# GNN layer with a routed mixture of experts: hidden sums kept and split in PSUM, four banks for the first layer, two for the second

## The reference, cut to what matters

```python
x = x + gnn(_layernorm(x), src, dst, edge_weight)       # N = 50000 rows of D = 256
# FFN: E = 8 experts, F = 1024, top-1 routing, capacity C = ceil(1.25 * N / E)
h = _layernorm(x)
probs = softmax(h @ gate_w + gate_b); idx = argmax(probs)
buf = rows of h gathered per expert (at most C each)
hmid = relu(buf @ w1[e] + b1[e])                        # [C, 1024]
ybuf = hmid @ w2[e] + b2[e]                             # [C, 256]
x = x + nan_to_num(ybuf[idx, pos] * prb * kept)
```

## Time and profile before

| what | value |
|---|---|
| median of three runs | 3566.1 us |
| the profiled execution: its own time | 3569.06 us |
| its span in the profile | 3567.3 us |
| mean granted TensorE clock, of full speed | 0.82 |
| PE busy | 2846.6 us (80%) |
| DVE busy | 2245.0 us (63%) |
| ACT busy | 1539.7 us (43%) |
| POOL busy | 1724.4 us (48%) |

### The profile page before, as it was taken

How to read it: one execution, slowest core, us unless ns; L and a number is a source line. 1 busy time by engine, 2 the same in 40 slices (tenths; PEclk the granted TensorE clock), 3 DMA queues, 4 the chain that set the end, 5 groups by cost and what they waited for, 6 DMA issues and landing times.

```text
span 3567.3 us, 60077 instructions
## 1 busy us (share of the span) xinstructions
PE 2846.6 (80%) x18806; PEld 2603.9 (73%) x18807; DVE 2245.0 (63%) x5836; ACT 1539.7 (43%) x2638; POOL 1724.4 (48%) x1183
## 2 busy tenths in 40 slices
PE   4553434067677777499999999999999999999998
PEld 3443433067676667399898999888999989998987
DVE  5645555076566566377666677676677776667666
ACT  2322222044444444255444555454455545554443
POOL 4788887635555566333434333343433343334323
PEclk8666666555555555699999999999999999999999
DMA  8544444388787776311211211121211121111111
GB/s 313 153 89 77 87 78 86 29 269 252 249 259 248 228 240 207 115 48 56 66 57 44 72 48 52 49 67 57 67 48 47 56 67 47 48 51 49 42 47 37
DMA packets 306007, 374.74 MB, mean 105 GB/s; under 512 B 34887, under 2 KB 266340, under 8 KB 302608
## 3 DMA queue, kind: packets, MB, share of 16 engines
q1 hardware_dynamic: 224608, 202.49, 19.3%
q0 software_dynamic: 77728, 145.22, 14.9%
q10 hardware_dynamic: 3600, 26.22, 1.8%
HBM read 185.42 MB, written 196.46 MB: 107 GB/s over the span
## 4 chain that ended last, share of the span: by engine, by line
PE 53%; DVE 4%; issue 1%; DVEq 0%; DMA 0%; SPq 0%; ACT 0%; POOL 0%; POOLq 0%; ACTq 0%
PE u_Y L1181 27%; PE u_H L1170 23%; PE u_T L1153 3%; DVE y L1110 1%; DVE yo L1129 1%; DVE yo L1126 1%; DVE y L1115 0%; DVE hn L1078 0%; DVE low L1120 0%; DVE hlo L1098 0%; DVE yo L1124 0%; DMA slots<-blank 0%; DMA u_pay<-slots 0%; DVE scales L1073 0%; DVEq L1078 0%
## 5 line engine op out<-in xcount | busy, mean ns | idle before, releaser
L1010 POOL DMA_INDIRECT out_x<-yo,u_token x348 | 668.5, 1921 | 1261.4 <-DVE yo L1131 1179.5
L1181 PE MATMUL u_Y<-whi,hhi 128*128 128x256 f32 x2784 | 784.2, 282 | 1.5 <-DVE hlo L1098 1.5
L1181 PE MATMUL u_Y<-wlo,hhi 128*128 128x256 f32 x2784 | 775.4, 279 | 0.0
L1181 PE MATMUL u_Y<-whi,hlo 128*128 128x256 f32 x2784 | 774.8, 278 | 0.0
L1046 ACT ACTIVATE hm<-u_H,b1e 128x512 f32<-128x512 f32 (+1 forms) x736 | 487.9, 663 | 639.8 <-PE u_H L1170 627.0
L539 POOL DMA_INDIRECT slots<-pay,slot_i x392 | 415.3, 1059 | 325.5 <-DVE slot_i L748 210.3
L1170 PE MATMUL u_H<-xhi,whi 128*128 128x512 f32 (+1 forms) x1472 | 563.6, 383 | 8.0 <-issue 5.5
L1170 PE MATMUL u_H<-xhi,wlo 128*128 128x512 f32 (+1 forms) x1472 | 562.2, 382 | 0.0
L1170 PE MATMUL u_H<-xlo,whi 128*128 128x512 f32 (+1 forms) x1472 | 560.2, 381 | 0.0
L1181 PEld LDWEIGHTS u_Y<-whi,hhi 128*128 128x128 f32 x2784 | 528.4, 190 | 1.7 <-DVE hlo L1098 1.7
L1181 PEld LDWEIGHTS u_Y<-wlo,hhi 128*128 128x128 f32 x2784 | 528.8, 190 | 0.0
(11 more groups left out here) (137 smaller groups left out, 3747.9 us busy)
## 6 DMA issues: line engine op xcount, KB each, us to landing
xt<-in_x SPq DMA_DIRECT2D x49, 1024.0 KB
out_x<-pay SPq DMA_DIRECT2D x49, 1024.0 KB
u_pay<-slots SPq DMA_DIRECT2D x93, 534.0 KB, 3.8
agg<-zeros ACTq DMA_DIRECT2D x25, 1024.0 KB
at<-agg SPq DMA_DIRECT2D x49, 512.0 KB
raw<-in_L_ffn_w POOLq DMA_DIRECT2D x14, 1024.0 KB
src_row<-in_src SPq DMA_DIRECT2D x25, 512.0 KB
slots<-blank SPq DMA_DIRECT2D x8, 801.0 KB, 5.1
```

What stands on the lines that cost most here:

```text
L1010: pool.indirect_dma_start(out=out[:, :], out_offset=bass.IndirectOffsetOnAxis(ap=token[:, s:s + 1], axis=0), in_=yo[:, s, :], in_offset=No ...
L1181: last = pe.matmul(ps_Y[:, s, 0:D], a[:, f, rows], w2_at(w, buf, f), start=(f == 0 and j == 0), stop=(f == KF - 1 and j == 2))
```

## The change

`u_H` gets four banks instead of two (`f % HID`, `HID` = 4), and `u_Y` two full banks instead of four half-used ones. The ReLU writes its result back into the bank of `u_H`, in place; the copy `hhi` and the subtraction `hlo` read it there, and the SBUF tile `hm` is gone. A bank of `u_H` is therefore free only when `hlo` of its step has been made, and PE waits for that (`hid_ready`) ahead of steps 4 to 7, and for nothing ahead of steps 0 to 3. In the second layer only the first matmul into each bank carries `start`. The addition of b2 is one instruction of 4·256 elements per partition in place of four of 256.

```diff
-    hm = sb("hm", [P, KF, UNIT], F32)
...
-    ps_H = ctx.enter_context(nc.psum_tensor("u_H", [P, 2, UNIT], F32))
-    ps_Y = ctx.enter_context(nc.psum_tensor("u_Y", [P, SUB, 512], F32))
+    ps_H = ctx.enter_context(nc.psum_tensor("u_H", [P, HID, UNIT], F32))
+    ps_Y = ctx.enter_context(nc.psum_tensor("u_Y", [P, SUB, D], F32))
...
-                        act.activation(hm[:, f, cols], ps_H[:, f % 2, cols], ACT.Relu, bias=b1e[:, f:f + 1])\
+                        act.activation(ps_H[:, f % HID, cols], ps_H[:, f % HID, cols], ACT.Relu, bias=b1e[:, f:f + 1])\
...
-                        act.activation(hhi[:, f, cols], hm[:, f, cols], ACT.Copy).then_inc(hhi_ready, 1)
+                        act.activation(hhi[:, f, cols], ps_H[:, f % HID, cols], ACT.Copy).then_inc(hhi_ready, 1)
...
-                        v.tensor_tensor(hlo[:, f, cols], hm[:, f, cols], hhi[:, f, cols].bitcast(F32), ALU.subtract)\
+                        v.tensor_tensor(hlo[:, f, cols], ps_H[:, f % HID, cols], hhi[:, f, cols].bitcast(F32), ALU.subtract)\
...
-                    for s in range(subs):
-                        last = v.tensor_tensor(y[:, s, :], ps_Y[:, s, 0:D], b2e[:], ALU.add)
-                    last.then_inc(y_read, 1)
+                    v.tensor_tensor(y[:, used], ps_Y[:, used], b2e[:].unsqueeze(1).broadcast_to([P, subs, D]), ALU.add)\
+                        .then_inc(y_read, 1)
...
-                        pe.wait_ge(relu_done, KF * u + (f - 1 + SEED["relu_done"]))
+                        if f >= HID:
+                            pe.wait_ge(hid_ready, KF * u + (f + 1 - HID + SEED["hid_ready"]))
...
-                                last = pe.matmul(ps_Y[:, s, 0:D], a[:, f, rows], w2_at(w, buf, f),
-                                                 start=(f == 0 and j == 0), stop=(f == KF - 1 and j == 2))
+                                last = pe.matmul(ps_Y[:, s, :], a[:, f, rows], w2_at(w, buf, f),
+                                                 start=(f == 0 and j == 0 and s % 2 == 0),
+                                                 stop=(f == KF - 1 and j == 2), skip_group_check=True)
```

More of the change, by code:

```diff
@@ L832, in run_experts @@
     HUGE = 1e4
+    HID = 4
+    assert D * 2 == 512
     def sb(name, shape, dt):
@@ L1165, in unit @@
                     for f in range(KF):
-                        pe.wait_ge(relu_done, KF * u + (f - 1 + SEED["relu_done"]))
+                        if f >= HID:
+                            pe.wait_ge(hid_ready, KF * u + (f + 1 - HID + SEED["hid_ready"]))
                         passes = [(w, a, k) for k in range(KD) for w, a in ((whi, xhi), (whi, xlo), (wlo, xhi))]
                         for j, (w, a, k) in enumerate(passes):
-                            last = pe.matmul(ps_H[:, f % 2, cols], w1_at(w, buf, k, f), a[:, k, cols],
+                            last = pe.matmul(ps_H[:, f % HID, cols], w1_at(w, buf, k, f), a[:, k, cols],
                                              start=(j == 0), stop=(j == len(passes) - 1))
```

## The result

| | before | changed |
|---|---|---|
| median | 3565.56 us | 4211.95 us |
| ratio to before, 95% interval | | 1.1817 (1.1795 to 1.1838) |
| profiled execution: own time / span | 3569.06 / 3567.3 us | 4212.22 / 4210.3 us |
| mean granted clock | 0.82 | 0.78 |
| PE busy | 80% | 72% |

The account below looks back on a forecast made before the run. The prediction took PE's matmuls to bound the kernel, 22.76 us per full unit. Its terms, 551 + 23 + 39 + 11 + 7 = 631 us, on the median of 3566.1 gave 4197 us, range 4130 to 4290 us.

Parts of the forecast that it names:

- t0: Time when DVE begins the addition of b2, the second layer of the unit before having ended; 22.76 us apart before.
- stall, full behind full: PE's step 4 waits for the first `hlo`, from t0 + 5.30 to t0 + 10.84: 5.54 us per unit.
- clock, full behind full: Lowered PE clock after each new pause, charged at the mean behind earlier 4.1 us pauses: 1.90 us, ends 1.52 and 2.80.
- 74 full units (with the 7 second ones): Full units following a full one: 74 × (5.54 + 1.90) = 551 us, plus 7 us for experts' second full units.
- 8 first half units: First half unit of each expert grows from 18.54 to 21.42 us, +2.9 each: 23 us.
- 7 full behind half: Full units following a half unit: stall 3.64 us, with the clock 5.5 each: 39 us.
- 2 second half units: Half units following a half unit, without a row of their own, charged 5.5 us each: 11 us.
- the 7 us for POOL in the second unit of an expert: First `hlo` at t0 + 11.53 instead of + 10.29 while POOL handles weights, no longer hidden: 7 us in all.
- Costs of nothing: ReLU and copy in PSUM, two `u_Y` banks, missing `start` flags and `hlo` reading PSUM were charged no time.
- The stall without the clock's fall: Rival: pauses come but the clock does not fall, 158 us given back, about 4039 us; chance 4%.
- A second fall per unit: Rival: the clock falls twice per unit, 1.90 us more in 92 units, +175, about 4372 us; chance 7%.
- Not slower: Rival: the first `hlo` ends before PE reaches step 4, so no stall, 3564 us; chance 2%.

Follow-up runs that it names:

- e1: Changed kernel with ReLU results kept in SBUF `hm` and PE's bank release by the ReLU instead of `hlo`: ratio 1.0011 to the kernel before.
- e2: Changed kernel with three banks of `u_H` instead of four: ratio 1.213 to the kernel before, 4325 us on 3565.56.
- e4: Changed kernel with DVE's `normalise` of the unit after next moved ahead of its wait for the second layer: ratio 1.1363 to the kernel before, 4052 us on 3565.56.
- e5: Changed kernel without DVE's replacement of NaN and infinities: ratio 1.0184 to the kernel before, 3631 us on 3565.56.
- e6: Changed kernel with most output work spread between the next unit's `hlo` subtractions and `normalise` two units ahead: ratio 1.0113 to the kernel before.
- e3: Changed kernel with 22 matmuls of unused result put ahead of PE's wait at step 4: ratio 1.1376 to the kernel before, 4056 us on 3565.56.
- e9: Changed kernel with every `hhi` copy done twice on ACT: ratio 1.1836 to the kernel before.
- e7: Kernel before (`hm`, two banks) with one b2 addition and most output work spread between the next unit's `hlo` subtractions, no early `normalise`: ratio 1.0006.
- e10: Kernel before with one b2 addition, output work spread between the next unit's `hlo` subtractions, and `normalise` two units ahead: ratio 0.9953.
- e11: As e10, with POOL's two weight-splitting instructions cut into eight pieces of 512 columns each: ratio 0.9924 to the kernel before.
- e12: The changed kernel repeated without alteration: ratio 1.1836 to the kernel before.
- e8: Changed kernel with the addition of b2 in four instructions again: ratio 1.1844 to the kernel before.

## Why the prediction was right

**The mechanism** was right in each step: the wait of step 4, DVE's whole output work in front of the `hlo` that ends it, the closed loop behind it, and one fall of the clock for each pause. e1 shows that nothing else in the change costs, e2 that the stall grows with PE's earlier arrival, e4 and e5 that it shrinks with DVE's queue, e6 that it vanishes when the queue is turned around, in all full units behind full ones but the six that meet POOL.

**The terms**, from t0 to t0 in the two profiles:

| term | forecast | measured |
|---|---|---|
| first `hlo` begins | t0 + 10.08 | t0 + 10.01 |
| stall, full behind full | 5.54 us | 5.44 us |
| clock, full behind full | 1.90 us | 7.92 − 5.44 = 2.48 us |
| 74 full units (with the 7 second ones) | 551 + 7 us | 74 × (30.68 − 22.87) = 578 us |
| 8 first half units | 23 us | 8 × (22.34 − 18.76) = 29 us |
| 7 full behind half | 39 us | 7 × (29.09 − 23.99) = 36 us |
| 2 second half units | 11 us | 2 × (17.99 − 13.56) = 9 us |
| sum | 631 us | 652 us |

(22.87 is the mean of the 74 before, 22.76 plus what the second and third unit of an expert took more. The spans of the two profiles differ by 643, 9 less than this sum: the first t0 came 8 us earlier in the changed run, at 1508.48 instead of 1516.59. The medians differ by 646.)

The mis-sized term is the clock's fall. The prediction charged 1.90 us, the mean behind pauses of 4.1 us, and said itself that the new pause is longer. Behind 5.3 us PE ran slow for 5.3 us in the unit shown, and its row of 0.66 is 2.7 us lost out of 8; the clock's record gives 2.42 us of lost work per unit over all 74. The upper end of the range, 2.80, held it. e3 gives the share by experiment: 2.2 us per full unit come back if PE is kept busy. The first half units show the same: their pause grew from 4.1 to 7.8 us and the clock's loss in work behind it from 1.9 to 2.6 us, where the prediction left it as before; that is most of the 6 us by which this term fell short. The Trainium skill (TensorE: Matmul & The Clock Gate, on why this matters for your kernels) tells to keep PE from idling between bursts because its clock then falls back to the lower level; the rows of the changed kernel and e3 agree.

**A term taken too high:** the 7 us for POOL in the second unit of an expert. In those units the first `hlo` began at t0 + 10.0 to 10.4, not 11.5. In expert 1 before, POOL's splitting ran from 1742.26 to 1757.34, across the t0 of that unit, 1754.69; in the changed kernel it ended at 1819.15, 4.9 us ahead of the t0, 1824.01.

**Luck in the sum.** That the forecast missed by only 15 us is in part luck, since larger errors cancel. Of the 21 us between 631 and 652, the clock was 74 × 0.58 = 43 us too low and the first half units 6; the stall was 7 us too high, POOL's term 7, and the other units 5, and the full units before had 8 us above 22.76 that the prediction did not subtract. The earlier first t0 of the changed run brought the 21 down to 15. The range's lower end, 4130, is 20 us below what its own bounds give, 4197 − 32 − 15 = 4150; nothing hung on it.

**Costs of nothing:** ACT was covered (e9), the waits for the ReLU had had no length (e1), `u_Y` in two banks cost nothing (e1). For `hlo` with an operand in PSUM the trace now has its own row:

```profile
L1099 DVE TENSOR_TENSOR hlo<-u_H,hhi 128x512 fp32r<-128x512 f32 x656 | 430.4, 686 | 451.2 <-ACT hhi L1051 441.0 <-issue 10.2
```

686 ns against 684 ns for the same instruction from SBUF in the unit of the earlier trace rows. The 65 ns more for a PSUM source that the prediction worked out, as an estimate, from the Trainium skill (VectorE: DVE Perf Modes, the section on the TRN2 errata) aren't seen; the measurement decides.

**The rivals.** The stall without the clock's fall (4039 us) is refuted for the changed kernel; e3, at 4056 us on the scale of 3565.56, is the kernel that it described. A second fall per unit (4372 us) was not seen: the clock's record has one in each of the 91 units. Not slower was never near.

## What to carry to other kernels

When a buffer's release moves from one engine to another, look at what is queued ahead of the new releaser on its engine, not at how long the release itself takes: here a subtraction of 0.69 us stood behind 10 us of output work. On an engine without slack, price a pause with the clock that it costs afterwards. And when an order is turned to close one pause, look for the work of other engines that the moved instructions will now meet.

## What the runs showed that was not expected

- ACT is a little faster with PSUM in the place of SBUF: the ReLU, which now writes PSUM, took 662 ns instead of 688, and the copy of `hhi`, which now reads it, 599 instead of 633 (by shape, 512 columns, 656 each). Nothing waited for it.
- POOL's indirect writes took 984 ns on average instead of 1921. Before, the one that began at 2016.77, beside the eight `hlo` with both operands in SBUF, took 5.14 us. It was one of 73 that took about 5 us, and e1, with `hm` in SBUF, has 73 of them too; in the changed kernel none took over 1.07 us, though 248 of 348 ran beside an `hlo`, which now has one operand in PSUM:

```profile
L1011 POOL DMA_INDIRECT out_x<-yo,u_token x348 | 342.5, 984 | 2252.4 <-DVE yo L1131 2170.5 <-issue 81.9
```

- DVE and POOL hold each other up for whole instructions. `hn` rose from 1.4 to 13.4 us (e7), two `hlo` from 1.3 to 13.1 us (e10), four products from 1.1 to 9.0 us (e6), each time ending within 1 us of POOL's splitting of weights. It goes the other way too: POOL's cast of weights beside the eight `hlo` of the earlier trace rows took 5.62 us, and 3.61 in the same place of the changed kernel, where `hlo` reads PSUM. The Trainium skill (SBUF — State Buffer, on who interferes with whom) says that the two engines share a pair of ports as an exclusive lock, taken by DVE for two SBUF inputs and in its two-port modes, and that whoever issues first keeps it for the whole instruction; these rows and e11 agree. The same section of the Trainium skill infers that a `tensor_tensor` takes nothing that POOL needs to issue a DMA; the 5.14 us against 0.98 above speak otherwise.
- A longer stall need not cost its full length. From e12 to e8 the stall grows by 0.19 us and the full unit by 0.08; from the changed kernel to e2 by 1.37 and by 1.16. What of the slow stretch falls into the pause is not paid for: in e2 that part of the clock's loss grew from 0.99 to 1.76 us.
